# Picked rows by indirect DMA, eight weight slots and a plain second product in a kernel with two expert layers

## The reference

```python
# layer 0, experts: 64 experts, two per token, H = 256, D = 512
probs = softmax(x @ Wg + bg); topk_vals, topk_idx = top_k(probs, 2)
h = relu(einsum('bsd,edh->bseh', x, W1) + b1)
expert_out = einsum('bseh,ehd->bsed', h, W2) + b2
out = einsum('bse,bsed->bsd', sparse_w, expert_out) + x      # then a layer norm with gamma, beta
# layer 1, graph attention, twice: W is 512 x 1024 (8 heads of 128), then 1024 x 512 (8 heads of 64)
h = (x @ W).reshape(N, heads, out_ch)
a_src = einsum('nhc,hc->nh', h, att_src); a_dst = einsum('nhc,hc->nh', h, att_dst)
# layer 1, experts: 8 experts, one per token, H = 256, D = 512
```

## Time and profile before

| | us |
|---|---|
| median of 3 runs | 1501.57 |
| lowest and highest | 1492.67, 1505.25 |
| the profiled execution: run | 1511.43 |
| the profiled execution: span | 1509.7 |

### The profile page before, as it was taken

One profiled execution on the slowest core, in us unless ns is written; L12 is line 12 of the kernel. 1 busy time (PEld: TensorE's weight loads), 2 busy tenths in 40 slices (PEclk: granted clock), 3 DMA queues, 4 the chain that ended last, 5 costly groups with the idle time before them and its releaser, 6 DMA issues. The chain is left out here.

```text
span 1509.7 us, 18794 instructions
## 1 busy us (share of the span) xinstructions
PE 1096.2 (73%) x5288; PEld 754.5 (50%) x5292; DVE 950.1 (63%) x1829; ACT 607.4 (40%) x835; POOL 581.9 (39%) x493
## 2 busy tenths in 40 slices
PE   3788768952478788778607899968999876816586
PEld 1343356741467777667303477858454421205473
DVE  6466576448345566565595689994277777464355
ACT  0322343230233343443111477767046767731231
POOL 0000044403668784000330576765066667601102
PEclk9999979965678899998758899979899988865697
DMA  2000000032488999998512111110211011001795
GB/s 87 0 0 1 0 1 0 0 122 79 151 262 276 304 299 295 298 305 280 169 40 72 42 43 29 54 32 15 72 42 43 28 49 42 14 1 36 260 322 185
DMA packets 118761, 164.20 MB, mean 109 GB/s; under 512 B 26357, under 2 KB 68925, under 8 KB 118698
## 3 DMA queue, kind: packets, MB, share of 16 engines
q1 hardware_dynamic: 101722, 124.37, 26.3%
q0 software_dynamic: 5600, 18.35, 3.8%
q10 hardware_dynamic: 11376, 20.71, 3.7%
HBM read 133.59 MB, written 29.82 MB: 108 GB/s over the span
## 5 line engine op out<-in xcount | busy, mean ns | idle before, releaser
L1339 POOL TENSOR_TENSOR am<-CT,qb 128x1024 f32<-128x1024 f32 x128 | 300.6, 2362 | 193.2 <-DMA qb<-q_scratch 110.3
L1438 DVE TENSOR_TENSOR am<-PS,am 128x1024 f32<-128x1024 f32 x128 | 156.6, 1223 | 53.3 <-ACT PS L1350 48.6
L1350 ACT ACTIVATE PS<-adb,ab 128x1024 f32<-128x1024 f32 x128 | 143.0, 1117 | 103.2 <-DVE am L1438 102.7
L973 PE MATMUL PS<-xgT,w1r 128*128 128x128 f32 x1264 | 179.1, 303 | 2.6 <-DMA w2r<-in_L_ffn_W 2.6
L973 PEld LDWEIGHTS PS<-xgT,w1r 128*128 128x128 f32 x1264 | 172.2, 219 | 4.1 <-DMA w2r<-in_L_ffn_W 3.4
L1422 DVE CUSTOM_DVE_ANT_0 masked<-PS,mask 128x1024 f32<-128x1024 f32 x128 | 156.1, 1220 | 27.8 <-issue 26.1
L1547 PE MATMUL PS<-PT,h 128*65 128x512 f32 x256 | 136.0, 679 | 37.3 <-ACT PT L1357 19.8
L1357 ACT ACTIVATE PT<-am,as 128x1024 f32<-128x1024 f32 x128 | 145.1, 1134 | 0.7 <-DVE am L1438 0.6
L1536 PEld LDWEIGHTS PS<-h,PT 128*128 128x128 f32 x1024 | 127.9, 206 | 11.3 <-ACT PT L1357 7.5
L1055 DVE TENSOR_TENSOR w2l<-w2r,w2h 128x1024 fp32r<-128x1024 f32 x79 | 105.6, 1337 | 43.5 <-ACT w2h L1023 42.4
L1536 PE MATMUL PS<-h,PT 128*128 128x129 f32 x1024 | 128.6, 289 | 5.5 <-ACT PT L1357 5.5
(11 more groups left out here) (288 smaller groups left out, 1852.4 us busy)
## 6 DMA issues: line engine op xcount, KB each, us to landing
w1r<-in_L_ffn_W SPq DMA_DIRECT2D x79, 512.0 KB, 5.3
w2r<-in_L_ffn_W SPq DMA_DIRECT2D x79, 512.0 KB, 6.9
ys_scratch<-yo ACTq DMA_DIRECT2D x79, 256.0 KB, 4.9
xg<-xs_scratch SPq DMA_DIRECT2D x71, 128.0 KB, 4.6
adb<-a_scratch SPq DMA_DIRECT2D x16, 512.0 KB, 3.7
qb<-q_scratch SPq DMA_DIRECT2D x16, 512.0 KB, 4.1
wc<-in_L_gnn_W POOLq DMA_DIRECT2D x16, 256.0 KB, 5.7
xg<-xs_scratch SPq DMA_DIRECT2D x15, 256.0 KB, 5.1
```

Of the source, the lines that this page charges most:

```text
L973: mm = pe.matmul(PS[:, 2 + j % 2, c * P:(c + 1) * P], w1r[:, j, k, c * P:(c + 1) * P], xgT[:, j % 2, k, :], start=(k == 0), stop=(k == KD ...
L1339: pool.tensor_tensor(am[:, k % RING, :], CT[:, s, :], qb[:, hd % 2, :], ALU.add).then_inc(s_sum, 1)
L1350: act.activation(RELU, adb[:, hd % 2, :], ACT.Relu, bias=ab[:, s, hd:hd + 1]).then_inc(s_relu, 1)
L1438: dve.tensor_tensor(am[:, k % RING, :], RELU, am[:, k % RING, :], ALU.add).then_inc(s_all, 1)
```

## The change

1. After routing of layer 0, DVE makes a table `rowsi` of 128 x 64 integers: row p, column e is off[e] + p if p is below first[e], and a number above every position otherwise. It replaces the tables `offi` and `firsti`.
2. In x0, POOL fetches rows with an indirect DMA by column e of this table, 128 indices each, and stores the outputs by the same column; indices out of bounds are skipped. SP loads only weights there, ACT stores nothing.
3. `w1r` and `w2r` have eight slots (WR = 8). SP waits for the end of e-4 and loads the weights of e+4; eight experts are prefetched during routing of layer 0. In x2, four blocks' weights are loaded first, then rows e and weights e+4 in turn.
4. The second product is two plain float32 matmuls of 512 columns. All work for the split operands is gone from ACT and DVE, in x0 and x2.
5. `attention_vectors` is gone. In the combine, SP loads the 16 chunks of W, PE transposes each (four transposes), ACT copies the result, and PE multiplies it by the transposed att vectors (four matmuls of 2 or 4 columns). These stand between the bias products of PE for tiles 3 to 7, four chunks at each.
6. Buffers move to make room. The loop over 64 experts is unrolled by eight instead of four.

```diff
@@ routing, vector
-                    link(dve.tensor_copy(offi[:], off[:]))
                     if not flat:
-                        link(dve.tensor_copy(sb["firsti"][:], first[:]))
+                        link(dve.tensor_scalar(beg[:], first[:], pcol[:], float(2 * N * K), ALU.is_le, ALU.mult))
+                        link(dve.scalar_tensor_tensor(beg[:], off[:], pcol[:], beg[:], ALU.add, ALU.add))
+                        link(dve.tensor_copy(sb["rowsi"][:], beg[:]))
@@ buffers
-        w1r = place("w1r", [P, 4, KD, H], F32, 112 * KIB)
-        w2r = place("w2r", [P, 4, HC, D], F32, 128 * KIB)
+        WR = 8
+        w1r = place("w1r", [P, WR, KD, H], F32, 112 * KIB)
+        w2r = place("w2r", [P, WR, HC, D], F32, 144 * KIB)
         def first_experts(sp):
-            for e in range(4):
+            for e in range(WR):
                 load_weights(sp, ins["L0_ffn_W1"], ins["L0_ffn_W2"], slice(e, e + 1), e, s_w0)
@@ experts, gpsimd
-                    pool.memset(xg[HALF:P, :, :], 0.0).then_inc(s_clear, 1)
+                    pool.memset(xg[:], 0.0).then_inc(s_clear, 1)
+                    if picked is None:
+                        return
+                    LAG = 6
+
+                    def fetch(e):
+                        wait(pool, s_t, e - 3)
+                        pool.indirect_dma_start(xg[:, e % 4, :], None, xs[0:rows, :], bass.IndirectOffsetOnAxis(
+                            picked[:, e:e + 1], 0), bounds_check=rows - 1, oob_is_err=False).then_inc(s_xg[e % 4], 16)
+
+                    def store(e):
+                        pool.wait_ge(s_ym, e + 1)
+                        pool.indirect_dma_start(ys[0:rows, :], bass.IndirectOffsetOnAxis(picked[:, e:e + 1], 0),
+                                                yo[:, e % 4, :], None, bounds_check=rows - 1, oob_is_err=False
+                                                ).then_inc(s_ys[e % 4], 16)
+
                     pool.wait_ge(s_clear, 1)
-                    if beside is not None:
-                        beside(pool)
+                    for e in range(blocks + LAG):
+                        if e < blocks:
+                            fetch(e)
+                        if e >= LAG:
+                            store(e - LAG)
@@ experts, sync
                     def body(e, g, j, last):
                         wait(sp, s_y, e - 3)
-                        row = first_row(sp, table, e, rows)
-                        load_rows(sp, e, row, j)
-                        if not fetched or not isinstance(e, int) or e >= 4:
-                            load_weights(sp, W1_d, W2_d, expert(sp, e), j, s_w)
-
-
+                        if picked is None:
+                            sp.dma_start(xg[:, j % 4, :], xs[bass.ds(first_row(sp, table, e, rows), P), :]
+                                         ).then_inc(s_xg[j % 4], 16)
+                        ahead = e + WR // 2
+                        if not isinstance(e, int):
+                            ahead = within(sp.snap(ahead), 0, blocks - 1)
+                        elif ahead >= blocks or fetched and ahead < WR:
+                            return
+                        load_weights(sp, W1_d, W2_d, expert(sp, ahead), (j + WR // 2) % WR, s_w)
+
+                    if not fetched:
+                        for e in range(WR // 2):
+                            load_weights(sp, W1_d, W2_d, expert(sp, e), e, s_w)
@@ experts, tensor
                     def output(e, j):
-                        pe.wait_ge(s_hl, e + 1)
-                        pe.wait_ge(s_wl, e + 1)
+                        pe.wait_ge(s_hm, e + 1)
                         wait(pe, s_ym, e - 1)
-                        products = [(hp, wp, c) for hp, wp in ((hTh, w2h), (hTh, w2l), (hTl, w2h)) for c in range(HC)]
-                        for n, (hp, wp, c) in enumerate(products):
-                            mm = pe.matmul(PS[:, 4 + j % 2, :], hp[:, j % 2, c, :], wp[:, j % 2, c, :],
-                                           start=(n == 0), stop=(n == len(products) - 1))
+                        for c in range(HC):
+                            mm = pe.matmul(PS[:, 4 + j % 2, :], hT[:, j % 2, c, :], w2r[:, j, c, :],
+                                           start=(c == 0), stop=(c == HC - 1))
@@ combine of layer 0, sync
+                sp.dma_start(att1[0:HEADS, :], ins["L1_gnn_att_src1"]).then_inc(s_att, 16)
...
+                for i, (name, k, c) in enumerate(chunks):
+                    if i >= 4:
+                        sp.wait_ge(s_wt, i - 3)
+                    sp.dma_start(wc[:, i % 4, :], ins[name][k * P:(k + 1) * P, c * 512:(c + 1) * 512]
+                                 ).then_inc(s_wc[i % 4], 16)
@@ combine of layer 0, tensor: in the loop over tiles, behind the bias product of tile t
+                    for i in range(4 * (t - 3), 4 * (t - 2)) if 3 <= t < 7 else ():
+                        if i + 1 < len(chunks):
+                            turned(i + 1)
+                        summed(i)
```

More of the change, by code:

```diff
@@ L782, in router_buffers @@
                     made["end"] = at
-                    at = at if scratch is None else scratch
+                    at = at if scratch is None else scratch[0]
                 for k, (shape, dt) in group.items():
+                    if k == "c0" and scratch is not None:
+                        at = scratch[1]
                     size = 2 if dt == BF16 else 4
@@ L835, in loop @@
         def loop(eng, body):
-            for j in range(4):
+            for j in range(WR):
                 body(j, 0, j, False)
-            with eng.Fori(1, NX0 // 4 - 1) as g:
-                for j in range(4):
-                    body(eng.snap(g * 4 + j), g, j, False)
-            for j in range(4):
-                body(NX0 - 4 + j, NX0 // 4 - 1, j, j == 3)
+            with eng.Fori(1, NX0 // WR - 1) as g:
+                for j in range(WR):
+                    body(eng.snap(g * WR + j), g, j, False)
@@ L891, in build, with experts @@
-        w2h = place("w2h", [P, 2, HC, D], F32R, 168 * KIB)
-        w2l = place("w2l", [P, 2, HC, D], F32R, 199 * KIB + 512)
-        hTh = place("hTh", [P, 2, HC, P], F32R, 42 * KIB)
-        hTl = place("hTl", [P, 2, HC, P], F32R, 44 * KIB)
-        def experts(tag, blocks, table, W1_d, W2_d, b1_d, xs, ys, rows, loop, s_w, fetched, owner=None,
-                    counts=None, beside=None):
+        def experts(tag, blocks, table, W1_d, W2_d, b1_d, xs, ys, rows, loop, s_w, fetched, owner=None, picked=None):
@@ L1012, in body @@
                         a.then_inc(s_hm, 1)
-                        act.wait_ge(s_hm, e + 1)
-                        act.copy(hTh[:, j % 2, :, :], hT[:, j % 2, :, :]).then_inc(s_hh, 1)
-                        if not last:
-                            upper(e + 1, g + 1 if j == 3 else g, (j + 1) % 4)
-                        if not (isinstance(e, int) and e == 0):
+                        if picked is None and not (isinstance(e, int) and e == 0):
                             store(e - 1, (j + 3) % 4)
-                    def upper(e, g, j):
-                        act.wait_ge(s_w[j], (g + 1) * 32)
-                        wait(act, s_y, e - 1)
-                        act.copy(w2h[:, j % 2, :, :], w2r[:, j, :, :]).then_inc(s_wh, 1)
                     def store(e, j):
@@ L1064, in body @@
                         if not (isinstance(e, int) and e == 0):
[L1065 to L1070 removed]
+                            moved(e - 1, g * (WR // 4) + (j - 1) // 4, (j + 3) % 4)
                     loop(dve, body)
@@ L1186, in _, with turned, summed @@
             def _(pe):
+                def turned(i):
+                    pe.wait_ge(s_wc[i % 4], 16 * (i // 4 + 1))
+                    if i >= 2:
+                        pe.wait_ge(s_wtm, i - 1)
+                    for b in range(4):
+                        mm = pe.transpose(PS[:, 5 + i % 2, b * P:(b + 1) * P], wc[:, i % 4, b * P:(b + 1) * P], ident[:])
+                    mm.then_inc(s_wt, 1)
+                def summed(i):
+                    name, k, c = chunks[i]
+                    pe.wait_ge(s_wtm, i + 1)
+                    for b in range(4):
+                        if name == "L1_gnn_W1":
+                            hd = 4 * c + b
+                            to = PS[:, 7, k * 2 * HEADS + hd:(k + 1) * 2 * HEADS:HEADS]
+                            by = att1T[:, hd:2 * HEADS:HEADS]
+                        else:
+                            at = (KD + k) * 2 * HEADS
+                            to = PS[:, 7, at:at + 2 * HEADS].rearrange("p (a h) -> p a h", a=2)[:, :, 2 * b:2 * b + 2]
+                            by = att2T[:, b, :]
+                        mm = pe.matmul(to, wct[:, i % 2, b * P:(b + 1) * P], by, start=True, stop=True)
+                    mm.then_inc(s_v, 1)
                 for t in range(NT):
```

167 lines of the change are left out of this document (78 added, 89 removed).

## The result

The changed kernel takes 1447.42 us (median of 4 runs, 1445.12 to 1456.98) against 1497.73 us for the kernel before on the same chip. The ratio is 0.9676, 95% interval 0.964 to 0.9712: faster by 3.2%. The forecast was 1402, with 1370 to 1445 as its range. The sign was right, the gain was half of what was forecast (50 us of 100), and the time lies just above the range.

The account below looks back on a forecast made before the run. Bytes, with a shallow queue, were taken to pace layer 0's experts: -107 there, +5 combine, +2 layer 1's blocks, -100 us in all, span 1509.7 to 1409.7, median 1402; range 1370 to 1445.

Parts of the forecast that it names:

- The bytes of the experts: Layer 0's 64 experts: 67.1 MB instead of 94.9, DMA share 0.97, stage 245 us, 107 less than 352.5.
- The depth of the queue: Layer 0's experts: seven to eight experts in flight instead of four nearly close DMA's gaps, share 0.84 to 0.97.
- POOL: Layer 0's experts: a gather and a scatter per expert cost 2.5 us of POOL, and neither waits.
- Rivals 3 and 4: Experts: POOL binds, 1432 us in all (0.08) or slower kernel (0.04); skipped rows cost like moved ones, near 1479 (0.08).
- PE in the experts: Layer 0's experts: two plain products at 0.88 us replace six at 1.56, body from 3.7 to about 3.1 us.
- hidden by DMA: Layer 0's experts: PE's saving does not show, since its 218 us stay under the 245 us of the transfers.
- the floor of 218 us: Layer 0's experts: PE's 64 bodies, 198 us, plus some 20 for wait for rows, low clock and tail.
- Rival 1: Layer 0's experts: picked rows burden only eight DMA engines, stage 270 us, whole kernel 1427 us; chance 0.25.
- Rival 2: Layer 0's experts: weights stream fast enough and PE sets the stage at 218 us, whole kernel 1375 us; chance 0.13.
- The combine: Layer 0's combine: 16 attention chunks at 1.8 us each on PE delay tile 7; +5 us, between 0 and +13.
- Layer 1's blocks: Layer 1's 15 expert blocks: four blocks' weights ahead of the first rows; +2 us, range -2 to +12.
- The offset: Whole kernel: the median lies below the profiled execution, so a span of 1409.7 becomes a forecast of 1402.

Follow-up runs that it names:

- half: The changed kernel with one of the two plain matmuls of the second product left out in both layers' experts; 1422.35 us, ratio 0.9446.
- four: The changed kernel with four weight slots instead of eight, weights and layer 1's rows fetched two ahead; 1452.30 us, ratio 0.9691.
- split0: The changed kernel with the split second product back in layer 0 only, DVE making the differences before it copies the output; 1451.61 us, ratio 0.9655.
- Again: The changed kernel measured once more, unaltered; 1458.44 us, ratio 0.9711.
- split8: The changed kernel with the split second product back in both layers, DVE making w2l after it copies the output; 1469.70 us, ratio 0.98.

## Why the prediction was wrong, point by point

- **The bytes of the experts: right.** 67.3 MB for 67.1, 3275 engine-us for 3404. With PE's work shortened (half), the stage was 233.6 us at a share of 0.87 over start and tail; the forecast for transfers was 245, with 213 of work in it, which is the same 0.87.
- **The depth of the queue: right in the gaps, not needed.** PE's waits for rows vanished, as forecast, but with four slots they vanish too (four).
- **POOL: right.** 128 indirect DMAs cost about 1.0 us each with 0.3 between, 2.6 us a pair for the forecast 2.5, and never set the pace. Skipped rows cost no bytes (8.45 MB for 8.4), and the queue's 443 engine-us stand against 409 forecast. Rivals 3 and 4 fall.
- **PE in the experts: the step that failed.** "Two plain float32 products of 512 columns cost 10.57 / 24 = 0.44 us each, 0.88 together" read a matmul's price off a record. The 24 records are 12 matmuls: of this kind the loop issues 64, and the trace holds 128 records. The two plain products cost 1.72 us, more than the six fp32r matmuls that they replace (1.56 in the earlier trace rows, 1.47 in split0), so the body rose to 3.94 us instead of falling to 3.1. The saving that was "hidden by DMA" was a loss, and the floor of 218 us was 269. This is 23.5 of the 33.7 us by which the span missed its forecast of 1409.7; 14.0 are the combine and 3.2 layer 1's blocks, and 7.0 went the other way, in stages where nothing was forecast (3.5 before the experts, 2.5 in attention, 1.0 at the end). The trace before could have told it. Its groups for the first and the second product of the experts read:

```profile
L973 PE MATMUL PS<-xgT,w1r 128*128 128x128 f32 x1024 | 145.3, 303 | 1.8 <-DMA w2r<-in_L_ffn_W 1.8
L983 PE MATMUL PS<-w2h,hTh 128*128 128x512 f32 x128 | 48.8, 464 | 1.3 <-DVE hTl L1067 1.3
```

  The loop issues eight plain matmuls an expert, 512 in all, and 1024 records stand there; of the fp32r ones it issues two of this kind an expert, 128, and 128 stand there. The Trainium skill (FP8 and Floating Point Precision, TensorE Precision Notes) says that true FP32 takes four passes through the array. The trace agrees as far as a ratio can: 0.86 us for a plain matmul of 512 columns against 0.23 for an fp32r one (0.47 us for two, 507.24 to 507.71 in split0) is 3.7 to 1. What the two records of a plain one stand for, the trace does not say.
- **Rival 1, rows on half of the engines: falls.** It gave 270 us for the stage, and the stage took 269, but that is coincidence: with PE relieved and the same bytes (half) it fell to 233.6. By that rival's own sum, with the engine time as measured (2832 / 16 + 443 / 8 = 232 us of work on the burdened engines, and 25 for start and end), it would have been over 250. And from 440 to 550 us of half the weights take 0.869 of all 16 engines' time and the rows 0.124. With the weights spread evenly and the rows on eight engines, these eight would be at 0.869 + 2 x 0.124 = 1.12, more than there is. So the rows were spread. The rule for a plain transfer that the prediction quotes does not show in these indirect ones.
- **Rival 2, PE as the floor: the right mechanism with a wrong price.** It had 0.13 of the chances at 218 us. It decided, at 269.
- **The combine: the same error.** The small products were priced at 13.82 / 64 us each, which are records too. They cost 1.56 us, not 0.86. A chunk of 2.45 for 1.8 us, four between two bias products, makes DVE wait 7 to 8 us for each of the last two tiles: +19 instead of +5, and 14.0 us of the miss.
- **Layer 1's blocks.** First transpose at 16.9 us, 11 later than before, as forecast ("some 10 us later"); the stage 91.6 for 88.4, in its range (-2 to +12). The sum had a slip: ahead of and with the rows of block 10 come the weights of 14 blocks and the rows of 11, 17.6 MB and not 18.6, which is 3 us less at its rate. What lengthens the stage was not found (see above), so the hit is in part luck.
- **The offset.** The forecast took 8 us off, from the profiled span to the median of the runs, because the profiled execution before lay above that median. The changed kernel's profiled span lay 4 us below its median instead. Again shows how large such differences can be: unaltered code differs by 16 us of span between two executions, 11 of them in attention. The range had no room for that; without it the miss is 34 us, with it 45.

## To carry to other kernels

Before a row is used as a price, divide its count by the number of instructions that the loop issues: a plain float32 matmul is two records here, and costs as much as almost four fp32r ones, so the split into three fp32r products is the cheaper one in this kernel (1.47 us for 1.72) as long as ACT and DVE make the halves in time (split8 against split0). A stage that waits for bytes hides such a loss, and it comes out with the very change that brings the bytes in time; so price the cover that remains on every engine, not only on the one that is relieved. And order work by who waits for it: twelve chunks ahead of four short products cost 12 to 13 us more than the same twelve behind them (all sixteen then cost 6 to 7).

## What was not expected of the hardware

- The granted clock stayed at 0.50, the lower of its two levels (1.2 GHz), from 659.2 to 704.0 us of the changed kernel, although PE was busy in all of it. What it did there were transposes of 128 columns, products of two or four, and three of the bias products (512 columns):

```profile
659.20:704.00 44.80, 44.80 (x195) 39.86 (x195) 31.27 (x35) 10.09 (x21) 20.63 (x19) 0.50 0.48 160
```

  A busy PE, as the profile counts it, is thus no warrant for the higher level. The Trainium skill (TensorE: Matmul & The Clock Gate, Part 1: The HAM clock gate) says that the gate follows how busy PE has been lately. If busy time in the profile is taken for that, this stretch does not agree; which of these instructions count for the gate, no run here shows.
- One VectorE instruction with three operands took 10.94 us at 673.04, while GpSimd added beta in eight instructions (9.83 us from 673.60, through at 683.4). It ended 0.6 us after them, at 684.0. So did the one of 9.60 us before, and in split0, where POOL was through at 669.2, DVE's lasted only 3.57 us, to 669.7. In all three, the length is that of POOL's remaining work and 0.6 us, and the changed kernel's instruction had even started 0.6 us ahead of POOL's first.
- ACT's copies of the third and fourth chunk came up to 6 us late in all six executions on two of the chips, with no releaser that the profile names, and not at all in the four on the third.
